# Gate product first in every step, and the convolution spread over 21 steps in threes

## What is computed

```python
xn = layernorm(u)
k[l, h] = real(sum_n W[h, n] * exp(dt[h] * Lam[n] * l))   # 128 taps for each channel
s = causal_conv(xn, k) + xn * D                            # along the sequence, per channel

def fp4_linear(x, w):                                      # both sides rounded to FP4 in blocks of 16
    return fp4_quant_dequant(x) @ fp4_quant_dequant(w).T

h = silu(fp4_linear(xn, w_gate)) * fp4_linear(xn, w_up)    # 256 -> 704
g = silu(fp4_linear(h, w_down))                            # 704 -> 256
out = u + s * g
```

## Time and profile before

| what | value |
|---|---|
| time before, median of 3 runs (lowest, highest) | 601.17 us (600.91, 601.51) |
| the profiled execution: its time, its span | 602.32 us, 600.5 us |
| PE busy | 478.5 us, 80% of the span |
| DVE busy | 547.2 us, 91% |
| ACT busy | 404.8 us, 67% |
| POOL busy | 199.2 us, 33% |
| mean granted TensorE clock | 0.964 of full speed |
| the chain that ended last | PE 49%, DVE 29%, issue 10%, POOL 5%, ACT 3%, DMA 2% |

### The profile page before, as it was taken

The page is one execution under the profiler, slowest core; times in us unless marked ns, Lnnn a source line. Parts: engine busy times, 40 slices in busy tenths (PEclk is TensorE's granted clock), DMA queues, the critical chain, the costliest instruction groups (busy, mean ns, idle before and its releaser), DMA issues.

```text
span 600.5 us, 13231 instructions
## 1 busy us (share of the span) xinstructions
PE 478.5 (80%) x4956; PEld 334.6 (56%) x4956; DVE 547.2 (91%) x689; ACT 404.8 (67%) x568; POOL 199.2 (33%) x302
## 2 busy tenths in 40 slices
PE   0000357678888899999999999999999888888874
PEld 0000333345556567777777777777777655655653
DVE  6999999889999999899999999999999998998794
ACT  6963856898888876666666666666666654655562
POOL 1093000655555551111111133333332477451400
PEclk9999957879999999999999999999999998989999
DMA  5980012242222345455555555555553399340134
GB/s 175 350 257 1 1 35 88 87 97 89 87 89 88 106 124 158 145 158 149 152 157 158 157 151 150 150 153 157 158 159 89 50 156 156 62 70 1 22 50 70
DMA packets 101186, 70.80 MB, mean 118 GB/s; under 512 B 8848, under 2 KB 100752, under 8 KB 101008
## 3 DMA queue, kind: packets, MB, share of 16 engines
q1 hardware_dynamic: 93072, 61.94, 34.6%
q0 software_dynamic: 8064, 8.13, 9.4%
HBM read 61.28 MB, written 16.91 MB: 130 GB/s over the span
## 4 chain that ended last, share of the span: by engine, by line
PE 49%; DVE 29%; issue 10%; POOL 5%; ACT 3%; DMA 2%; SPq 0%; DVEq 0%; ACTq 0%; POOLq 0%
PE ps L1221 23%; PE ps L1239 8%; PE ps L1241 4%; PE ps L1230 4%; DVE work L854 4%; PE ps L1254 4%; PE ps L1258 3%; DVE wgu L941 3%; DVE work L849 3%; DVE work L888 2%; DVE work L880 2%; DVE sm L796 2%; PE ps L1209 1%; POOL gbuf L506 1%; DVE xh L916 1%
## 5 line engine op out<-in xcount | busy, mean ns | idle before, releaser
L1221 PE MATMUL ps<-wgu,work 128*128 128x512 f16 (+1 forms) x1152 | 247.5, 371 | 7.3 <-DVE work L880 6.1
L1221 PEld LDWEIGHTS ps<-wgu,work 128*128 128x128 f16 x1152 | 113.9, 100 | 119.9 <-issue 17.1
L605 ACT ACTIVATE work<-ps,con 128x704 f32<-128x704 f32 x64 | 54.2, 847 | 116.4 <-PE ps L1221 116.4
L600 ACT COPY work<-ps 128x1408 f16<-128x1408 f16 x64 | 84.9, 1327 | 11.0 <-PE ps L1230 10.7
L1239 PE MATMUL ps<-wdh,work 128*128 128x256 f16 x704 | 89.5, 277 | 2.1 <-ACT work L600 1.4
L849 DVE SCALAR_TENSOR_TENSOR work<-work 128x960 f32<-128x960 bf16 (+2 forms) x67 | 74.0, 1123 | 11.8 <-ACT work L620 11.8
L506 POOL TENSOR_TENSOR gbuf<-gbuf,xh 128x256 f32<-128x256 f32 (+1 forms) x42 | 39.8, 1018 | 107.4 <-DVE work L862 100.1
L1230 PE MATMUL ps<-id,work 128*128 128x128 f16 x704 | 51.0, 222 | 30.1 <-DVE work L888 28.5
L1239 PEld LDWEIGHTS ps<-wdh,work 128*128 128x128 f16 x704 | 66.9, 99 | 10.2 <-ACT work L600 1.6
L854 DVE SCALAR_TENSOR_TENSOR work<-work 128x1920 f16<-128x1920 bf16 (+3 forms) x36 | 69.8, 1939 | 1.2
L815 DVE TENSOR_TENSOR work<-work,ps 128x960 f32<-128x960 f32 (+2 forms) x63 | 68.4, 1126 | 1.1
(11 more groups left out here) (153 smaller groups left out, 662.0 us busy)
## 6 DMA issues: line engine op xcount, KB each, us to landing
work<-kpad SPq DMA_DIRECT2D x64, 512.0 KB, 4.0
work<-L_attn_u SPq DMA_DIRECT2D x33, 256.0 KB, 4.8
gbuf<-u_rev SPq DMA_DIRECT2D x4, 2048.0 KB, 17.9
out<-gbuf POOLq DMA_DIRECT2D x7, 1024.0 KB, 9.3
out<-L_attn_u SPq DMA_DIRECT2D x1, 768.0 KB, 5.8
out<-gbuf POOLq DMA_DIRECT2D x1, 768.0 KB, 8.1
work<-L_ffn_w_down SPq DMA_DIRECT2D x1, 704.0 KB, 7.9
work<-L_ffn_w_gate SPq DMA_DIRECT2D x1, 640.0 KB, 4.4
```

The lines of the kernel that those rows point to most:

```text
L600: nc.scalar.copy(hT[par], src).then_inc(hT_a, 1)
L1221: last = T.matmul(p_gu[:, a:b], xT[par][:, t, c, :], wgu[:, part, c % 2, a:b], start=(n == 0), stop=(n == len(todo) - 1))
```

## The change

Five things change; all of them are orders and counts, no operation is added or removed.

1. The 32 groups run in steps 8 to 28: two in an even step, one in an odd step, so three in two steps. `groups_before(it)` is the first group of step `it`, `groups_of(it)` their number. Steps 8 to 27 are ten passes of ACT's loop (PAIRS = 10), and step 28 (S_TAIL) takes the last two groups.
2. PE's step has one order: `h_transpose(0)`, `gate_up(0)`, `x_transpose`, first half of a group, `down` of the tile before, second half, `gate_up(1)`, `h_transpose(1)`, then, in a step of two groups, the first half of the second group, `down`, its second half. `gate_up(0)` stood behind a `down`, and in convolution steps `gate_up(1)` behind the second `h_transpose`.
3. ACT's step has one order: both squares stand together, the silus of the down product stand later, `x_copy` behind both squares.
4. SP loads filters in the same rhythm, four and two a step.
5. `OPEN` of the three parts becomes 18, 23 and 28 (it was 16, 20, 24), and the limit of `some_gated` goes from S_OUT = 24 to OPEN[2] = 28. The gate products (`gated`) and the accumulating DMAs therefore sit in other steps: the seven accumulating DMAs that POOL issues inside the steps were two each in steps 24 and 25 and one each in 26, 27 and 30; now they are two each in steps 28, 29 and 30 and one in step 31. An eighth follows the last step both times.

```diff
-        S_CONV, S_OUT = NP // 4, NP // 4 * 3
+        S_CONV = NP // 4
+        PAIRS = (H // G8) // 3
+        S_TAIL = S_CONV + 2 * PAIRS
+        def groups_before(it):
+            return min((it - S_CONV) // 2 * 3 + (it - S_CONV) % 2 * 2, H // G8) if it > S_CONV else 0
+        def groups_of(it):
+            return groups_before(it + 1) - groups_before(it)
-        OPEN = [S_CONV + (S_OUT - S_CONV) * q1 // NQ for q0, q1 in PARTS]
+        OPEN = [min(it for it in range(NP) if groups_before(it + 1) >= q1 * C2 // G8) for q0, q1 in PARTS]
...
-                    some_gated(it, 4 if it < S_OUT else 8)
+                    some_gated(it, 4 if it < OPEN[2] else 8)
...
# ACT
                 if td:
                     h_copy(it * 2 - 4, 0)
-                    if td1:
-                        if a2:
-                            after(act, a_lp, it * 2 - 4)
-                        silu_out(it * 2 - 5, 1, 1 - par)
...
                 square(it, 1 - par, x, ch, 0)
-                if cv and xt:
-                    x_copy(it + 1, 1 - par)
                 if ch:
                     square(it, 1 - par, x, ch, 1)
-                if xt and not cv:
+                if td and td1:
+                    if a2:
+                        after(act, a_lp, it)
+                    silu_out(it * 2 - 5, 1, 1 - par)
+                if xt:
                     x_copy(it + 1, 1 - par)
+                if cv:
+                    y_copy(c0)
                 if xn:
                     x_norm(it + 3, 1 - par)
-                if td:
-                    if a2:
-                        act.wait_ge(a_lp, it * 2 - 2)
-                    silu_out(it * 2 - 4, 0, par)
-                if cv:
-                    y_copy(it * 2 - 2 * S_CONV)
-                if td and cv:
-                    h_copy(it * 2 - 3, 1)
                 if gu:
                     silu_gate(it * 2 + 1)
-                if td and not cv:
+                if td:
                     h_copy(it * 2 - 3, 1)
...
+                if td:
+                    if a2:
+                        act.wait_ge(a_lp, it)
+                    silu_out(it * 2 - 4, 0, par)
                 if ch:
                     down_scale(it - 1, 1 - par)
-                if cv:
-                    y_copy(it * 2 - 2 * S_CONV + 1)
+                if cv == 2:
+                    y_copy(c0 + 1)
...
# PE
                     h_transpose(it * 2 - 4, 0, par, copied=min(it + 1, NP))
-                    if it > 2:
-                        down(it * 2 - 5, 1)
                 if gu:
                     gate_up(it * 2, 0, par, it + 1)
                 if x:
                     x_transpose(it + 1, 1 - par)
                 if cv:
                     pe.wait_ge(a_lp, NT // 4)
-                    conv(it * 2 - 2 * S_CONV, 0)
-                if td:
-                    down(it * 2 - 4, 0)
+                    conv(groups_before(it), 0)
+                if td and it > 2:
+                    down(it * 2 - 5, 1)
                 if cv:
-                    conv(it * 2 - 2 * S_CONV, 1)
-                if gu and not cv:
+                    conv(groups_before(it), 1)
+                if gu:
                     gate_up(it * 2 + 1, 1, par, None)
                 if td:
                     h_transpose(it * 2 - 3, 1, par, copied=it + 2 if x else None)
-                if gu and cv:
-                    gate_up(it * 2 + 1, 1, par, None)
-                if cv:
-                    conv(it * 2 - 2 * S_CONV + 1, 0)
-                    conv(it * 2 - 2 * S_CONV + 1, 1)
+                if cv == 2:
+                    conv(groups_before(it) + 1, 0)
+                if td:
+                    down(it * 2 - 4, 0)
+                if cv == 2:
+                    conv(groups_before(it) + 1, 1)
```

More of the change, by code:

```diff
@@ L428, in _ @@
             load_t(1, 1)
[L429 removed]
+            with sp.Fori(0, PAIRS - 1) as q:
                 for par in range(2):
                     load_x(q * 2 + (S_CONV + par + 3), 1 - par)
[L432 to L434 removed]
+                    for k in range(4 - 2 * par):
+                        load_t(q * 6 + (4 * par + k + 2), k % 2)
+            for it in range(S_TAIL - 2, NP - 3):
                 load_x(it + 3, (it + 1) % 2)
[L436 removed]
+                for n in range(2 * groups_before(it) + 2, min(2 * groups_before(it + 1) + 2, H // 4)):
                     load_t(n, n % 2)
[L439 to L440 removed]
+            for n in range(2 * groups_before(NP - 3) + 2, H // 4):
+                load_t(n, n % 2)
             for n in range(2):
@@ L534, in some_gated @@
                 ready = [(n, part) for n, part in todo if 4 * n + 3 <= it * 2 - 5 and it >= OPEN[part]]
-                for n, part in sorted(ready, key=(lambda job: (job[1], job[0])) if it < S_OUT else None):
+                for n, part in sorted(ready, key=(lambda job: (job[1], job[0])) if it < OPEN[2] else None):
                     room -= 2 if part == 0 else 1
@@ L752, in _ @@
             act.wait_ge(con_ok, 1)
-            with act.Fori(0, (S_OUT - S_CONV) // 2) as q:
+            with act.Fori(0, PAIRS) as q:
                 for par in range(2):
-                    step(q * 2 + (S_CONV + par), par, True, True, True, True, True, True, cv=True)
-            with act.Fori(0, (NP - 4 - S_OUT) // 2) as q:
-                for par in range(2):
-                    step(q * 2 + (S_OUT + par), par, True, True, True, True, True, True)
-            step(NP - 4, 0, True, True, True, True, True, True)
-            step(NP - 3, 1, True, True, False, True, True, True)
+                    step(q * 2 + (S_CONV + par), par, True, True, True, True, True, True, cv=2 - par, c0=q * 3 + 2 * par)
+            for it in range(S_TAIL, NP - 2):
+                step(it, it % 2, True, True, it < NP - 3, True, True, True, cv=groups_of(it), c0=groups_before(it))
             step(NP - 2, 0, False, True, False, True, True, True)
@@ L1259, in conv, with step @@
                 last.then_inc(cv_h, 1)
-            def step(it, par, x, gu, td, cv=False):
+            def step(it, par, x, gu, td, cv=0):
                 if td:
```

13 lines of the change are left out of this document (3 added, 10 removed).

## The result

The changed kernel takes **587.17 us** (median of four runs, 586.48 to 588.45), the kernel before 601.31 us beside it: a ratio of **0.9768** (95% interval 0.9749 to 0.9787), 14.1 us less. The forecast was 585.8 with a range of 582.3 to 591.6. One execution of the kernel before, run beside e4, e6, e7 and e10, took 796.77 us at a mean granted clock of 0.677 and is left out of all ratios.

What follows compares the result with a forecast made beforehand. It took PE to bound the convolution steps, DVE the earlier ones. Terms 14.4 + 1.3 - 0.3 = 15.4 us off the profiled 602.32 gave 586.9, and 1.15 less for the median 585.8 us, range 582.3 to 591.6.

Steps and rivals of the forecast that it cites:

- Two steps of three groups cost PE 29.32: Convolution steps: PE's work for a two-group and a one-group step takes 29.32 us a pair instead of 30.7.
- The 0.98 by which a two-group step moves the gate product: Convolution steps: a two-group step starts the gate product 0.98 us later relative to DVE's step, a one-group step 0.42 earlier.
- The room: Convolution steps: the first gate product may start up to 1.06 us after DVE's step before DVE waits; before, about nil.
- lock-step: Rival, convolution steps: without that room each step costs its longer engine, 29.74 a pair, 4.2 us more, 590.0; chance 0.22.
- The 0.65 wait: Convolution steps: DVE's 0.65 us wait before the second L849, for ACT's square behind a copy, goes as the squares follow each other.
- Steps 8 to 28: The convolution steps of the changed kernel: 14.4 us less, with step 29 beginning at 520.6 instead of 535.0.
- the allowance for the first group and a late filter: Steps 8 to 28: 0.5 us added for the first group's wait for POOL's last input piece and a late filter.
- Steps 29 to 31: Last three steps: POOL's tables late, gate product earlier; 16.5, 12.3 and 12.6, sum 41.4 against 42.67, 1.3 us less.
- Behind the last step: After step 31: `down` starts later, waiting for `silu_out` behind two squares; 0.3 us more, taken between 0 and 1.4.
- Steps 0 to 7 at nothing: Steps before the convolution: DVE sets them, so no change in time was counted.
- The sum: Whole kernel: 14.4 + 1.3 - 0.3 = 15.4 us less than the profiled execution before.
- The clock as the slower rival: Rival, steps from 8 on: new PE waits drop the clock to 0.50, 1.6 us a step, eleven falls making it slower; chance 0.03.

Runs made afterwards that it cites:

- e4: Changed kernel, but in the step behind the last one ACT makes the silu of the down product ahead of the squares; 587.04 us, ratio 0.9779.
- e6: The kernel before, unchanged, in another profiled execution; 601.25 us.
- e7: Against e1, only ACT's two squares put together, with the old PE order and old silus kept; 596.85 us, ratio 0.9938 against the kernel before.
- e10: Changed kernel with POOL's last six gate products (step 31) each cut to one channel pair, so the output is incomplete; 585.64 us, ratio 0.975.
- e5: Changed kernel with PE's down of the tile before again ahead of the first gate product, ACT keeping the new order; 603.62 us, ratio 1.0059.
- e3: Changed kernel with ACT's copy of the input transposes back between the two squares, in convolution steps alone; 589.93 us, ratio 0.983.
- e2: Kernel before, with its two groups a step and gate plan, given the new orders of PE and ACT; 594.04 us, ratio 0.9901.
- e1: Changed kernel's 21-step convolution and gate plan, but PE and ACT in the orders of the kernel before; 601.16 us, ratio 1.0006.

## Why the prediction was right, and where it was off

- **Two steps of three groups cost PE 29.32.** 29.29 measured, from step 11 to 28. The durations read from start to start held, `down` and the gate product included. (The 0.98 by which a two-group step moves the gate product should have been 15.37 - 14.37 = 1.00, which changes nothing.)
- **The room.** A first gate product that starts at 0.66 and 1.64 in turn was predicted, it starts at 0.61 and 1.62. The wait of DVE was put at 0.5 and is 0.44. With `down` ahead of the gate product the pairs take 29.88 to 29.94 (e7, e5), so the room is worth 5.9 us; lock-step would have cost 4.2 by the reckoning, 5.9 by the run.
- **The 0.65 wait.** It goes, as predicted. That it is a matter of ACT's order alone was not in the sum but in my expectation of e3, and was wrong: with the copy between the squares it also needs a gate product that starts later than about 0.5 into the step (7.8 less 7.3, e3).
- **Steps 8 to 28.** 15.1 us less instead of 14.4. Of this 0.5 is the allowance for the first group and a late filter, which wasn't needed: steps 8 to 10 took 14.34, 14.60 and 14.35.
- **Steps 29 to 31.** That POOL's tables are the late thing was right: L891 waits 2.13 us for L498 and starts 13.70 into step 29, where 13.3 was predicted. All three steps were a little longer than put (42.2 against 41.4), so the term is 0.5 less instead of 1.3. The 13.70 lies inside the bounds of 12.1 to 14.9 and 0.2 above the 13.5 that the Trainium skill's rule (page "SBUF — State Buffer", section "Who interferes with whom") gave. POOL's operation of 32 elements took 2.19 us beside DVE's rounding (L485 at 527.50), which agrees with it.
- **Behind the last step: the term that was mis-sized.** 0.3 was taken between 0 and 1.4, and it is 1.7, outside the bounds. The step "the next tile's transposes and PE's waits for DVE's last roundings take most of this" held for the orders alone: e2, which has them without the gate products at this place, takes 23.03 us there, 0.2 more than before. It left out that the six gate products, which the change moves here, lengthen DVE's own work by 1.2 us (e10). e1, which has them with the orders of before, takes 23.66, 0.9 more. Both together give 1.7, in a trace that alone of these three has the lower clock among PE's work there.
- **Steps 0 to 7 at nothing.** 2.0 less were measured in one execution; step 2 differs by 0.9 between two executions of the kernel before (e6). Only the 0.4 of steps 3 to 7 is the change.
- **The sum was partly luck.** 15.4 was forecast for the profiled executions and 15.8 measured, but the terms miss by more: steps 0 to 7 and 8 to 28 gave 2.7 more than put, the last three steps and the end 2.2 less.
- **The clock as the slower rival.** It reads 1.00 in all steps from 8 to 31. The falls in steps 24 to 29 of before (two in each of its two traces, about 2.9 us in the first, 2.1 in the second) are gone: a gain that I had counted as the length of these steps without naming its cause. So in these traces some 2 to 3 of the 14 us are clock. Why it stays up is open. PE's waits for h do not decide it alone: steps 3 to 7 of before have 1.7 us of PE idle each and steps 25 and 26 of e2 have 2.2, all at 1.00, while e3, with PE's new order, has a fall in step 30 (0.87 there). Behind the last step, where PE waits 4.08, it falls again, in the 2 us after that wait:

```profile
568.00:570.00 2.00, 1.59 (x8) 0.81 (x6) 1.93 (x5) 0.37 (x1) 0.00 (x0) 0.50 0.83 77
```

- **The slower side does exist, in another place than the one priced.** e5 is 0.6% slower than before with only one of the moves undone. A half-done order is what costs there, not the clock, which reads 1.00 in all its steps from 3 to 31.

## What to carry to other kernels

Where two engines are nearly equally busy, look for both limits before changing one: balancing the work alone brought 0 us here, the order alone 6, both 14. How far one engine may run ahead of the other (here 1.06 us by the rows of before, from the time at which a buffer is freed to the time at which its result is wanted) decides whether uneven steps cost their mean or the longer engine in each. A product that is moved to an engine off the critical path, behind the last step, is not free if it runs beside the engine that the end waits for: price its neighbours too.

## What the runs showed of the hardware

**POOL and DVE hold each other up, in both directions.** The prediction had only the one: POOL's CAST of 240 elements 2.19 us beside a rounding against 0.38. The other: two passes of DVE over 704 elements take 2.46 us beside POOL's products of 512 and 1.69 without (e10). The rule of the Trainium skill named above says that either one can be the later, blocked one; both are seen here. The same two passes with one operand in PSUM are not lengthened beside POOL's products, as in step 30 of the changed kernel, in order of time (POOL, then DVE):

```profile
536.87 2.06 POOL L516 TENSOR_TENSOR gbuf<-gbuf,xh 128x256 f32<-128x256 f32 x2
...
537.69 1.69 DVE L818 TENSOR_TENSOR work<-work,ps 128x704 f32<-128x704 f32 x2
```

**An accumulating DMA that POOL issues takes about 1 us of POOL's own queue.** In the traces of before and after, the next POOL operation starts 0.96 to 1.16 us after such an issue begins (13 issues), and a table's first small operation directly behind one takes 0.86 to 1.19 us instead of 0.21. That this lengthening comes from the issue is not shown: in step 27 of before the same operation stood directly behind a product and took 0.85. At the start of step 29's tables, in order of time:

```profile
526.32 1.10 POOL L483 TENSOR_SCALAR sm<-sm 128x2 int32<-128x2 int32 x1
```

**The lower clock moves.** From step 2 on, the same kernel was slowed by it in steps 2, 27 and 29 in one execution and in 2, 26 and 28 in another; against the other trace such a step from 24 on was 0.8 to 1.6 us longer. Two single traces can't show a gain of 1 us in such a step.
